# A decoder kernel: the experts' low-rank output in two float32r products instead of one float32 product, and the loading and splitting of its matrix

## The chip, the cores and the metric

The kernel runs on one core of a Trainium2 chip. The metric is the device time of one execution, in microseconds (us). In the profile PE is the matrix engine (TensorE), DVE is VectorE, ACT is ScalarE, POOL is GpSimd, and SP is SyncE, which here only issues DMAs.

## What is computed

Two decoder layers on 1024 tokens of 512 features. Of the six sublayers the third one matters here, a dense layer with experts of low rank: each token picks one of four ranks (8, 16, 32, 64) by its gate scores, and the output of the first that many rows of `A` and columns of `B` is added to the dense product.

```python
def _L0_ffn_ref(hidden_states, W, b, A, B, gate_w, gate_b):
    RANKS = (8, 16, 32, 64)
    out = jnp.einsum('bsd,od->bso', hidden_states, W) + b
    x = hidden_states.reshape(-1, d_in)
    scores = x @ gate_w.T + gate_b
    probs = jax.nn.softmax(scores, axis=-1)
    routing_weights, selected = jax.lax.top_k(probs, TOPK)
    routing_weights = routing_weights / jnp.sum(routing_weights, axis=-1, keepdims=True)
    lora_outputs = jnp.stack([x @ A[:r, :].T @ B[:, :r].T for r in RANKS], axis=1)
    sel = jnp.take_along_axis(lora_outputs, selected[:, :, None], axis=1)
    final = jnp.sum(sel * routing_weights[:, :, None], axis=1)
    return out + final.reshape(bsz, seq, -1)
...
x = _layernorm(x + _L0_attn_ref(...), axis=-1)
x = _layernorm(x + _L0_xattn_ref(ctx_4096, ctx_4096, x), axis=-1)
x = _layernorm(x + _L0_ffn_ref(x, ...), axis=-1)
x = _layernorm(x + _L1_attn_ref(x, ...), axis=-1)
...
```

## The kernel before

Every engine runs a list written out by hand, and the engines meet at semaphores alone; nothing is scheduled. The tokens lie in eight blocks of 128 (`NT` = 8); a block's activations are 128 partitions by 512 columns. A float32 matmul of 512 columns appears in the trace as two records, a float32r one (written F32R, `fp32r` in the trace) as one.

**The second stage** (the second attention, `_L0_xattn`) ends with a loop of t from 0 to 9. Near its end PE already runs `ranks` (L872, the product with `A` and the gate weights, `agT`) and `ffn_W` (L882, the dense product) for blocks 0 and 1. SyncE issues in that loop the keys' rows to DRAM (`keys_out`, L520), scales (L487) and codes (L481) for the quantized weights.

**The third stage** is a loop of t from 0 to 7 on each of PE, ACT and DVE.

On PE, in this order: `lora_T(t)` (L886) turns the 128 x 64 matrix of the chosen rank products; for t < 4, two products of the next layer's low-rank matrices (L901), from t = 3 one of the next layer's combined attention matrix (L912, L913); `ffn_W(t + 2)` up to block 6, and block 7's at t = 7; `ranks(t + 2)`; `lora_out(t)` (L890), which adds the low-rank output and the bias onto the dense product in its bank; and from t = 2 the four transposes of block t - 2 (L606). At t = 7 `attention_out(0)` (L926 to L928, twelve float32r products) stands in as well. There are three banks for the dense product (`FF_BANK`), so `ffn_W(b)` for b of 3 and more waits for `ln_sum`, that is for DVE's addition (L1804) of block b - 3.

On DVE, in each t: from t = 3 the low half of a transposed block (`x_low`, L1810); for t < 4 two additions of the low-rank matrices (L1974); a `stack_low` step at t = 1, 2 and 4 (L1980, L1982, L1987); steps of unpacking the quantized weights (L1739, L1745, L1757, 128 x 1024 each); `choose(t + 2)` (L1960, L1961, L1962, L1965), which turns the gate scores into a mask and multiplies the rank products by it; from t = 3 `m_low` (L1998); then the wait for `lora_out(t)` and the addition and statistics of block t (L1804, L1788, L1789). Inside `choose` each step is "linked": it waits on a semaphore that the one before gives at its end, as each reads what that one wrote.

On ACT, in each t: `lora_T_out(t)` (L1450) copies the turned matrix to `lmT`; the bends of the quantized codes (L1224, L1226, L1232, L1240); `norm_tail` (L1281), which waits for POOL; `m_high_of` (L1440); and `x_T_out` (L1274), which copies a transposed block and is what `x_low` waits for.

PE's transposes of block b wait for `xl_ready` of b, that is for `x_low` of block b - 1 (one bank serves all of them).

Of the kernel before, what the change touches and what calls it, by code (L numbers as in the profile page):

```python
# [11 lines left out]
F32R = mybir.dt.float32r  # L12
# [123 lines left out]
def decoder_kernel(nc, i, out):  # L136
# [4 lines left out]
    with ctx:  # L141
# [28 lines left out]
        ad_st = sb("ad_st", [STACK, FF], F32R)  # L170
        folded_m = sb("folded", [P, T])
# [17 lines left out]
        lmT = sb("lmT", [P, 2, P])  # L189
        probT = lmT  # L190
# [26 lines left out]
        agT, at = carve(arena, at, KD * (RMAX + NL))  # L217
        bT0, at = carve(arena, at, D)
        wk3_at = at
        wk3, at = carve(arena, at, D)  # L220
        bT_d, at = carve(arena, at, D)
        wk2, at = carve(arena, at, D)
# [8 lines left out]
        lm, w_at = carve(early_w, w_at, 2 * RMAX)  # L231
        assert w_at <= 2 * CH
# [4 lines left out]
        lora_l = wo0  # L237
        ad_high = wh[:, :, :].rearrange("p s c -> p (s c)")[:, 0:FF]
# [65 lines left out]
        def turn_bank(n):  # L304

            return bank[(n + 1) % 2]
# [135 lines left out]
        def _(sp):  # L442
# [93 lines left out]
            sp.dma_start(bT0[0:RMAX + 1, :], i["bT0"]).then_inc(in_ffn0, 16)  # L536
# [5 lines left out]
            for t in range(2, NT):  # L542
                keys_out(t)
                if t % 2 == 0:
                    load_scales(C_O + t // 2)
                    load_codes(C_O + 1 + t // 2)
            load_scales(C_O + NT // 2)
# [54 lines left out]
        def _(pe):  # L602
# [259 lines left out]
            def ranks(b):  # L862
                pe.wait_ge(xt_ready, NT + b + 1)
                if b == 0:
                    pe.wait_ge(in_ffn0, 48)
                    pe.wait_ge(kq_ready, NT - 1)
                elif b == 1:
                    pe.wait_ge(kq_ready, NT)
                if b >= 2:
                    pe.wait_ge(lmT_ready, b - 1)  # L870
                for k in range(KD):
                    last = pe.matmul(turn_bank(b)[:, 0:RMAX + NL], xT[:, k, b * P:(b + 1) * P], agT[:, k, :],  # L872
                                     start=(k == 0), stop=(k == KD - 1))
                last.then_inc(ag_ps, 1)
# [343 lines left out]
        def _(act):  # L1218
# [226 lines left out]
            def lora_T_out(b):  # L1445
# [4 lines left out]
                nc.scalar.activation(lmT[0:RMAX, b % 2, :], turn_bank(b)[0:RMAX, P:2 * P], ACT.Copy).then_inc(lmT_ready, 1)  # L1450
# [273 lines left out]
        def _(dve):  # L1724
# [96 lines left out]
            nc.vector.memset(lmT[RMAX:RMAX + 1, :, :], 1.0)  # L1821
# [131 lines left out]
            def choose(b):  # L1953
# [22 lines left out]
            def stack_low_of(part):  # L1976

                dve.wait_ge(stack_hi, part + 1)
# [5 lines left out]
            def down_stack_low():  # L1984

                dve.wait_ge(stack_hi, 4)
                nc.vector.tensor_tensor(ad_st[2 * RG:STACK, :], a_down[2 * RG:STACK, :], f32(ad_high[2 * RG:STACK, :]), ALU.subtract).then_inc(stack_low, 1)  # L1987

            def b_lower(j):

                dve.wait_ge(stack_hi, 4 + j + 1)
# [17 lines left out]
            turn_norm(2 * NT - 1)  # L2009
            choose(1)  # L2010
# [243 lines left out]
def layout(a):  # L2254
# [42 lines left out]
    def pairs(m):  # L2297
# [7 lines left out]
        "bT0": np.concatenate([f["L0_ffn_B"].T[rank_at], f["L0_ffn_b"][None]]), "g_b": np.array([[gate_b[n] for n in LOGITS]], np.float32),  # L2305
# [28 lines left out]
```

## Time and profile before

| | us |
|---|---|
| median of 3 runs | 644.88 |
| the runs | 644.25 to 645.72 |
| the profiled execution | 645.23 |
| its span, first to last instruction | 643.1 |
| PE busy in it | 632.0 |
| DVE busy in it | 396.3 |
| ACT busy in it | 381.6 |

The span is what the trace shows; 2.1 us of the profiled execution lie around it. Busy times are those of each engine by itself; they overlap. In the timelines a DVE operation's length includes its last part, in which the next one may already start if it waits for nothing, so the step from start to start tells what a row takes.

### The profile page before, as it was taken

Reading aid. Unit: us, or ns where it says so; the run is one execution under the profiler, and the core shown is the slowest. Engines: PE = TensorE matmul, PEld = TensorE weight load, DVE = VectorE, ACT = ScalarE, POOL = GpSimd, SP = SyncE. Lnnn points to the kernel's source line nnn. Section 1 sums busy time; section 2 is a strip of 40 time slices with the busy share of each in tenths; the row PEclk is TensorE's granted clock in tenths of the full one; section 3 lists DMA queues with packets and bytes.
Section 4 is the critical chain, followed back from the end, with each engine's and each line's share of the span. In section 5 each row is a group of like instructions: output and inputs, shape, how many; then the busy total and the mean of one; then the engine's idle time right before and its main releaser. Section 6 shows DMA issues by size and latency. Waiting matters only on the chain.

```text
span 643.1 us, 8521 instructions
## 1 busy us (share of the span) xinstructions
PE 632.0 (98%) x3226; PEld 470.0 (73%) x3226; DVE 396.3 (62%) x633; ACT 381.6 (59%) x527; POOL 65.0 (10%) x116
## 2 busy tenths in 40 slices
PE   9999999999999999999999999999999999999996
PEld 6655555544558888888888888887777888888874
DVE  4798787667988777767667355335655212125467
ACT  2977789976987697576675154223565343316532
POOL 1032142311330000000000000001211000000012
PEclk9999999999999999999999999999999999999999
DMA  7771585512253134233320003056010322100002
GB/s 246 288 243 52 188 268 172 162 52 92 81 152 120 39 110 139 73 104 111 94 83 2 1 1 131 1 216 274 1 33 2 115 77 88 33 1 0 1 33 99
DMA packets 25590, 63.92 MB, mean 99 GB/s; under 512 B 5541, under 2 KB 10725, under 8 KB 24782
## 3 DMA queue, kind: packets, MB, share of 16 engines
q1 hardware_dynamic: 23294, 61.68, 29.4%
q10 hardware_dynamic: 2256, 1.70, 0.8%
q8 instruction: 26, 0.43, 0.3%
q14 instruction: 14, 0.11, 0.1%
HBM read 58.77 MB, written 4.60 MB: 99 GB/s over the span
## 4 chain that ended last, share of the span: by engine, by line
PE 88%; DVE 4%; ACT 4%; DMA 1%; issue 1%; SPq 1%; POOL 0%; POOLq 0%; DVEq 0%; ACTq 0%
PE bank L1043 18%; PE bank L1031 8%; PE bank L1030 8%; PE bank L1032 8%; PE bank L1122 8%; PE bank L1121 8%; PE bank L882 4%; PE bank L802 3%; PE bank L606 3%; PE bank L741 2%; PE bank L1097 1%; DMA codes<-in_c_qkv 1%; PE bank L912 1%; PE bank L926 1%; PE bank L984 1%
## 5 line engine op out<-in xcount | busy, mean ns | idle before, releaser
L1232 ACT ACTIVATE line<-line 128x1024 f32<-128x1024 f32 x87 | 91.4, 1050 | 0.2
L1030 PE MATMUL bank<-xh,wh 128*128 128x512 f32 x224 | 87.5, 391 | 0.0
L1031 PE MATMUL bank<-xl,wh 128*128 128x512 f32 x224 | 87.5, 391 | 0.0
L1032 PE MATMUL bank<-xh,wl 128*128 128x512 f32 x224 | 87.3, 390 | 0.0
L1043 PE MATMUL bank<-wh,xh 128*128 128x512 f32 x192 | 76.1, 396 | 0.2 <-DVE xl L2128 0.2
L1043 PE MATMUL bank<-wh,xl 128*128 128x512 f32 x192 | 74.9, 390 | 0.0
L2211 DVE SCALAR_TENSOR_TENSOR arena<-bank,ff_s,arena 128x512 f32<-128x512 f32 x28 | 21.0, 752 | 72.9 <-PE bank L1122 63.8
L2128 DVE TENSOR_TENSOR xl<-arena,xh 128x1024 fp32r<-128x1024 f32 (+1 forms) x26 | 29.7, 1141 | 35.4 <-ACT xh L1536 35.3
L1121 PE MATMUL bank<-xh,wh 128*128 128x512 f32 x128 | 50.3, 393 | 0.0
L1536 ACT ACTIVATE xh<-arena 128x1024 fp32r<-128x1024 f32 (+1 forms) x26 | 25.6, 991 | 41.3 <-PE bank L1043 34.8
L1122 PE MATMUL bank<-xl,wh 128*128 128x512 f32 x128 | 49.9, 390 | 0.0
L1032 PEld LDWEIGHTS bank<-xh,wl 128*128 128x128 f32 x224 | 42.1, 188 | 8.8
L1030 PEld LDWEIGHTS bank<-xh,wh 128*128 128x128 f32 x224 | 42.1, 188 | 8.5
L1031 PEld LDWEIGHTS bank<-xl,wh 128*128 128x128 f32 x224 | 42.1, 188 | 8.5
L1630 ACT ACTIVATE arena<-bank,ff_s 128x512 f32<-128x512 f32 x28 | 19.2, 686 | 43.4 <-PE bank L1122 43.4
L1512 ACT ACTIVATE arena<-bank 128x512 f32<-128x512 f32 x28 | 16.4, 586 | 46.9 <-PE bank L1032 46.9
L1695 POOL TENSOR_TENSOR rstd<-rstd,minus_half 128x1 f32<-128x1 f32 x40 | 26.7, 668 | 172.1 <-DVE rstd L2149 162.4
L1043 PEld LDWEIGHTS bank<-wh,xh 128*128 128x128 f32 x192 | 36.1, 188 | 8.3 <-DVE xl L2128 0.6
L1043 PEld LDWEIGHTS bank<-wh,xl 128*128 128x128 f32 x192 | 36.1, 188 | 7.5
L1121 PE MATMUL bank<-xh,wl 128*128 128x512 f32 x96 | 37.6, 391 | 0.0
L1745 DVE SCALAR_TENSOR_TENSOR line<-line 128x1024 f32<-128x1024 f32 x29 | 35.3, 1218 | 3.6 <-ACT line L1232 3.2
L1043 PE MATMUL bank<-wl,xh 128*128 128x512 f32 x96 | 37.4, 390 | 0.0
(219 smaller groups left out, 1264.3 us busy)
## 6 DMA issues: line engine op xcount, KB each, us to landing
codes<-in_c_gu SPq DMA_DIRECT2D x14, 512.0 KB, 3.8
scales<-in_s_gu SPq DMA_DIRECT2D x28, 256.0 KB, 4.0
codes<-in_t_gu SPq DMA_DIRECT2D x8, 512.0 KB, 4.2
codes<-in_c_dn SPq DMA_DIRECT2D x7, 512.0 KB, 4.6
scales<-in_s_dn SPq DMA_DIRECT2D x14, 256.0 KB, 3.9
fold<-in_t_dn SPq DMA_DIRECT2D x1, 3584.0 KB, 15.7
codes<-in_c_qkv SPq DMA_DIRECT2D x6, 512.0 KB, 4.8
scales<-in_t_gu SPq DMA_DIRECT2D x6, 512.0 KB, 3.8
```

The costliest lines, as they stand in the source:

```text
L882: pe.matmul(bank[FF_BANK[b % 3]][:, :], xT[:, k, b * P:(b + 1) * P], w0T[:, k, :], start=(k == 0), stop=False)
L1030: pe.matmul(dst, wh[:, s, c:c + P], xh[:, k, cols], start=(k == 0), stop=False)
L1031: pe.matmul(dst, wh[:, s, c:c + P], xl[:, k, cols], start=False, stop=False)
L1032: last = pe.matmul(dst, wl[:, s, c:c + P], xh[:, k, cols], start=False, stop=(k == KD - 1))
L1043: ins = pe.matmul(dst, h[:, b * P:(b + 1) * P], w, start=first and p == 0, stop=last and p == len(hiddens) - 1)
L1121: pe.matmul(dst, w[:, c:c + P], xh[:, k, cols], start=(k == 0), stop=False)
L1122: last = pe.matmul(dst, w[:, c:c + P], xl[:, k, cols], start=False, stop=(k == KD - 1))
L1232: nc.scalar.activation(below(slot), below(slot), ACT.Prelu, bias=bias, scale=scale, alpha=alpha).then_inc(bent, 1)
L1536: nc.scalar.activation(dst[:, cols], hT[:, j, cols], ACT.Copy).then_inc(done, 1)
L1695: last = nc.gpsimd.tensor_tensor(rstd[:, m % 2, 1:2], rstd[:, m % 2, 0:1], minus_half[:, :], ALU.pow)
L1745: nc.vector.scalar_tensor_tensor(weight(slot), weight(slot), -NEAR_UP, below(slot), ALU.max, ALU.subtract).then_inc(joined, 1)
L2128: nc.vector.tensor_tensor(low[:, cols], hT[:, j, cols], f32(hi[:, cols]), ALU.subtract).then_inc(done, 1)
```

## The change

The product `lora_out` is made of two float32r products instead of one float32 product. For that both its operands are split into a high part, rounded to float32r, and a low part, the rest.

- DVE: `choose` ends with three linked steps where it had one: the masked product, a cast of it to float32r (`lm_high`), and the difference, so that 128 columns stand side by side: 64 low, 64 high. PE turns all 128 in `lora_T`.
- ACT: `lora_T_out` makes two copies, `lm_both` (128 rows, low above high) and `lm_one` (the high rows again, above rows of ones). Once, before the third stage, it writes the rows of ones (after a wait for the DMAs that send `folded`, whose place `lm_one` takes), and `experts_high` rounds the two stacked copies of the matrix `B`.
- DVE, once: `experts_low`, two subtractions, between `choose(0)` and `choose(1)`.
- PE: `lora_out` is `lm_both` by `b_both` (low by high and high by low) and `lm_one` by `b_high_one` (high by high, and the bias as a high and a low row).
- SyncE: the load of `bT0` (65 x 512) behind `w0T` goes; `b_two` (128 x 512) and `b_one` (97 x 512) are loaded at t = 4 of the second stage's loop, behind `load_codes`.
- The count of `stack_hi` is one higher for all later waits. `lmT` is no longer shared with `probT`.

```diff
@@ block.sync
-            sp.dma_start(bT0[0:RMAX + 1, :], i["bT0"]).then_inc(in_ffn0, 16)
...
+                if t == KD:
+                    sp.dma_start(b_two, i["b_two"]).then_inc(in_ffn0, 16)
+                    sp.dma_start(b_one[0:ONE_ROWS.stop, :], i["b_one"]).then_inc(in_ffn0, 16)
@@ block.tensor
             def ranks(b):
-                    pe.wait_ge(in_ffn0, 48)
+                    pe.wait_ge(in_ffn0, 64)
...
-                pe.transpose(turn_bank(b)[0:RMAX, P:2 * P], lm[:, b % 2, :], ident[:, :]).then_inc(lm_ps, 1)
+                pe.transpose(turn_bank(b)[:, P:2 * P], lm[:, b % 2, :], ident[:, :]).then_inc(lm_ps, 1)
...
             def lora_out(b):
                 pe.wait_ge(lmT_ready, b + 1)
-                pe.matmul(bank[FF_BANK[b % 3]][:, :], lmT[0:RMAX + 1, b % 2, :], bT0[0:RMAX + 1, :], start=False, stop=True).then_inc(f0_ps, 1)
+                if b == 0:
+                    pe.wait_ge(lm_ready, 2)
+                pe.matmul(bank[FF_BANK[b % 3]][:, :], lm_both[:, b % 2, :], b_both, start=False, stop=False)
+                pe.matmul(bank[FF_BANK[b % 3]][:, :], lm_one[0:ONE_ROWS.stop, b % 2, :], b_high_one[0:ONE_ROWS.stop, :], start=False, stop=True).then_inc(f0_ps, 1)
@@ block.scalar
+            def experts_high():
+
+                act.wait_ge(in_ffn0, 64)
+                nc.scalar.activation(b_both, b_two, ACT.Copy)
+                nc.scalar.activation(b_high_one[0:ONE_ROWS.stop, :], b_one[0:ONE_ROWS.stop, :], ACT.Copy).then_inc(stack_hi, 1)
+
             for t in range(1, NT + 2):
+                if t == NT + 1:
+                    experts_high()
...
-                nc.scalar.activation(lmT[0:RMAX, b % 2, :], turn_bank(b)[0:RMAX, P:2 * P], ACT.Copy).then_inc(lmT_ready, 1)
+                nc.scalar.activation(lm_both[:, b % 2, :], turn_bank(b)[:, P:2 * P], ACT.Copy)
+                nc.scalar.activation(lm_one[0:RMAX, b % 2, :], turn_bank(b)[RMAX:P, P:2 * P], ACT.Copy).then_inc(lmT_ready, 1)
+
+            act.wait_ge(kb_out, 16 * KD)
+            for n in range(2):
+                nc.scalar.activation(lm_one[ONE_ROWS, n, :], ident[ONE_ROWS, :], ACT.Identity, bias=1.0, scale=0.0)
@@ block.vector
-            nc.vector.memset(lmT[RMAX:RMAX + 1, :, :], 1.0)
...
-                nc.vector.tensor_tensor(lm[:, s, :].rearrange("p (r m) -> p r m", m=SEG), ps[:, 0:RMAX].rearrange("p (r m) -> p r m", m=SEG),
-                                        mask.unsqueeze(1).to_broadcast([P, RMAX // SEG, SEG]), ALU.mult).then_inc(lm_ready, 1)
+                chosen, high = lm[:, s, 0:RMAX], lm_high[:, s, RMAX:P]
+                link(nc.vector.tensor_tensor(chosen.rearrange("p (r m) -> p r m", m=SEG), ps[:, 0:RMAX].rearrange("p (r m) -> p r m", m=SEG),
+                                             mask.unsqueeze(1).to_broadcast([P, RMAX // SEG, SEG]), ALU.mult))
+                link(nc.vector.tensor_copy(high, chosen))
+                nc.vector.tensor_tensor(chosen, chosen, f32(high), ALU.subtract).then_inc(lm_ready, 1)
+
+            def experts_low():
+
+                dve.wait_ge(stack_hi, 1)
+                low, row = slice(RMAX, P), slice(RMAX + ROWG, RMAX + ROWG + 1)
+                nc.vector.tensor_tensor(b_both[low, :], b_two[low, :], f32(b_both[low, :]), ALU.subtract)
+                nc.vector.tensor_tensor(b_high_one[row, :], b_one[row, :], f32(b_high_one[row, :]), ALU.subtract)
...
             choose(0)
             turn_norm(2 * NT - 1)
+            experts_low()
             choose(1)
```

The order of the instructions on the engines, at the places that matter. On DVE, t = 0 of the third stage, `choose(2)` and the addition of block 0, before:

```order
L1960 TENSOR_TENSOR gate_v<-bank,g_b 128x48 [waits ag_ps]
L1961 TENSOR_REDUCE gate_v<-gate_v 128x16 [waits dve_step]
L1962 TENSOR_TENSOR gate_v<-gate_v 128x8 [waits dve_step]
L1965 TENSOR_TENSOR early_w<-bank,gate_v 128x64 [waits lm_ps,dve_step]
L1804 TENSOR_TENSOR rbuf<-x,bank 128x512 [waits ln_done,f0_ps]
L1788 BN_STATS st<-rbuf 128x6 [waits ln_sum]
L1789 BN_AGGR mv<-st 128x2 [waits dve_step]
```

and in the changed kernel, where `early_w` is the place of `lm` and `wl` that of `lm_high`:

```order
L1987 TENSOR_TENSOR gate_v<-bank,g_b 128x48 [waits ag_ps]
L1988 TENSOR_REDUCE gate_v<-gate_v 128x16 [waits dve_step]
L1989 TENSOR_TENSOR gate_v<-gate_v 128x8 [waits dve_step]
L1993 TENSOR_TENSOR early_w<-bank,gate_v 128x64 [waits lm_ps,dve_step]
L1995 CAST wl<-early_w 128x64 [waits dve_step]
L1996 TENSOR_TENSOR early_w<-early_w,wl 128x64 [waits dve_step]
L1832 TENSOR_TENSOR rbuf<-x,bank 128x512 [waits ln_done,f0_ps]
L1816 BN_STATS st<-rbuf 128x6 [waits ln_sum]
L1817 BN_AGGR mv<-st 128x2 [waits dve_step]
```

The cast and the subtraction stand between the masked product and the addition of block 0, and the cast and the subtraction each wait for the step ahead of them. The same holds at each of the eight `choose` steps.

On PE, the third stage from `ranks(2)` to the dense product of block 3, before:

```order
L872 MATMUL bank<-arena 128x112 [waits lmT_ready,xt_ready]
L872 MATMUL bank<-arena 128x112 x3
L890 MATMUL bank<-arena,lmT 128x512 [waits lmT_ready]
L886 MATMUL bank<-ident,early_w 64x128 [waits lm_ready]
L901 MATMUL bank<-early_w,arena 128x512 [waits af_added]
L901 MATMUL bank<-early_w,arena 128x512
L882 MATMUL bank<-arena 128x512 [waits ln_sum]
```

and in the changed kernel (`early_w` under `ident` is the matrix that `lora_T` turns):

```order
L884 MATMUL bank<-arena 128x112 [waits lmT_ready,xt_ready]
L884 MATMUL bank<-arena 128x112 x3
L904 MATMUL bank<-arena_r,lm_both 128x512 [waits lm_ready,lmT_ready]
L905 MATMUL bank<-arena_r,lm_one 128x512
L898 MATMUL bank<-ident,early_w 128x128 [waits lm_ready]
L916 MATMUL bank<-early_w,arena 128x512 [waits af_added]
L916 MATMUL bank<-early_w,arena 128x512
L894 MATMUL bank<-arena 128x512 [waits ln_sum]
```

The one product on `lmT` became two, and block 0's waits for `lm_ready` too; the rest stands as it stood.

On ACT, the end of the second stage and the start of the third, before:

```order
L1274 ACTIVATE arena<-bank 128x4x128 [waits xt_ps]
L1232 ACTIVATE line<-line 128x1024 [waits bent]
L1274 ACTIVATE arena<-bank 128x4x128 [waits xt_ps]
L1450 ACTIVATE lmT<-bank 64x128 [waits lm_ps]
L1224 ACTIVATE line<-codes 128x1024 [waits joined,in_codes0]
```

and in the changed kernel:

```order
L1289 ACTIVATE arena<-bank 128x4x128 [waits xt_ps]
L1247 ACTIVATE line<-line 128x1024 [waits bent]
L1403 ACTIVATE arena_r<-arena 128x512 [waits in_ffn0]
L1404 ACTIVATE arena_r<-arena 97x512
L1289 ACTIVATE arena<-bank 128x4x128 [waits xt_ps]
L1478 ACTIVATE lm_one<-ident 33x128 [waits kb_out]
L1478 ACTIVATE lm_one<-ident 33x128
L1473 ACTIVATE lm_both<-bank 128x128 [waits lm_ps]
L1474 ACTIVATE lm_one<-bank 64x128
L1239 ACTIVATE line<-codes 128x1024 [waits joined,in_codes0]
```

`experts_high` stands ahead of the copy of block 7's transposes, the rows of ones behind it, ahead of `lora_T_out(0)`.

## Rows read from the trace of the kernel before

**Rows 1.** The page's busy time of each engine: time, share of the span, instructions.

```profile
PE 632.0 (98%) x3226; PEld 470.0 (73%) x3226; DVE 396.3 (62%) x633; ACT 381.6 (59%) x527; POOL 65.0 (10%) x116
```

**Rows 2.** Stretches of the third stage: length, busy time by engine, PEclk, DMA.

```profile
137.30:161.00 23.70, 23.70 (x85) 11.54 (x84) 19.27 (x36) 17.55 (x23) 4.95 (x9) 1.00 0.30 90
161.00:182.50 21.50, 21.36 (x78) 11.31 (x76) 20.53 (x36) 20.83 (x27) 7.09 (x8) 1.00 0.34 103
...
190.00:216.50 26.50, 26.22 (x138) 21.41 (x137) 22.01 (x32) 18.15 (x29) 0.79 (x2) 1.00 0.36 105
```

**Rows 3.** The chain of waits, 118 to 220 us: start, length, what.

```profile
137.31 0.87 PE bank L890 x2
138.30 1.06 PE bank L901 x4
139.36 3.63 PE bank L882 x8
...
187.88 0.23 PE bank L928
```

**Rows 4.** DVE's timeline at block 2's choice: start, length, operation [idle before].

```profile
137.35 0.21 DVE L1960 TENSOR_TENSOR gate_v<-bank,g_b 128x48 f32<-128x48 f32 x1 [0.71 <-PE bank L872]
...
137.83 0.17 DVE L1962 TENSOR_TENSOR gate_v<-gate_v 128x8 f32<-128x8 f32 x1
138.03 0.22 DVE L1965 TENSOR_TENSOR early_w<-bank,gate_v 128x64 f32<-128x64 f32 x1
138.22 0.69 DVE L1804 TENSOR_TENSOR rbuf<-x,bank 128x512 f32<-128x512 f32 x1
```

**Rows 5.** The same timeline of DVE at blocks 3 and 4.

```profile
142.92 1.23 DVE L1739 SCALAR_TENSOR_TENSOR line<-line 128x1024 f32<-128x1024 f32 x1
144.06 0.20 DVE L1960 TENSOR_TENSOR gate_v<-bank,g_b 128x48 f32<-128x48 f32 x1
...
151.52 0.68 DVE L1804 TENSOR_TENSOR rbuf<-x,bank 128x512 f32<-128x512 f32 x1
152.23 0.69 DVE L1788 BATCH_NORM_STATS2 st<-rbuf 128x6 f32<-128x512 f32 x1
```

**Rows 6.** PE's timeline, the dense product of block 5.

```profile
152.83 3.70 PE L882 MATMUL bank<-arena 128*128 128x512 f32 x8
```

**Rows 7.** DVE's timeline from 156 to 182 us.

```profile
156.14 1.23 DVE L1745 SCALAR_TENSOR_TENSOR line<-line 128x1024 f32<-128x1024 f32 x1
161.10 0.21 DVE L1960 TENSOR_TENSOR gate_v<-bank,g_b 128x48 f32<-128x48 f32 x1 [3.73 <-PE bank L872]
...
168.37 2.02 DVE L1987 TENSOR_TENSOR ad_st<-a_down,wh 32x1792 fp32r<-32x1792 f32 x1
170.49 0.21 DVE L1960 TENSOR_TENSOR gate_v<-bank,g_b 128x48 f32<-128x48 f32 x1
...
177.64 0.20 DVE L1960 TENSOR_TENSOR gate_v<-bank,g_b 128x48 f32<-128x48 f32 x1
...
181.71 0.68 DVE L1810 TENSOR_TENSOR xl<-bank,xh 128x512 fp32r<-128x512 f32 x1
```

**Rows 8.** PE's timeline, the transposes of block 4 at 182 us.

```profile
182.54 0.63 PE L606 MATMUL bank<-ident,x 128*128 128x128 f32 x4 [0.19 <-DVE xl L1810]
```

**Rows 9.** DVE's groups by form: busy time and mean ns of one.

```profile
L1844 DVE COPY project<-bank 128x64 f32<-128x64 f32 x8 | 1.2, 215 | 0.0
...
L1817 DVE COPY fold<-ident 128x128 f32<-128x128 f32 x1 | 0.2, 227 | 0.0
```

**Rows 10.** Timeline of ACT at 131 us.

```profile
131.67 0.60 ACT L1274 ACTIVATE arena<-bank 128x512 f32<-128x512 f32 x1 [3.23 <-PE bank L606]
```

**Rows 11.** Timeline of DVE, the idle stretch before 132.9 us.

```profile
132.89 1.28 DVE L1974 TENSOR_TENSOR arena<-arena,bank 128x512 f32<-128x512 f32 x2 [4.20 <-PE bank L901]
```

**Rows 12.** SyncE's own queue: when its DMAs were issued.

```profile
106.88 0.57 SPq L481 DMA_DIRECT2D codes<-in_c_dn  x1
111.38 5.26 SPq L520 DMA_DIRECT2D kq<-heads  x2
```

More of the change, by code:

```diff
@@ L170, in decoder_kernel @@
         ad_st = sb("ad_st", [STACK, FF], F32R)
+        with nc.sbuf_tensor("lm_one", [P, T], F32R) as lm_one:
+            pass
         folded_m = sb("folded", [P, T])
@@ L188, in decoder_kernel @@
         gate_v = sb("gate_v", [P, 2, NL + 3 * SEG])
-        lmT = sb("lmT", [P, 2, P])
-        probT = lmT
+        with nc.sbuf_tensor("lm_both", [P, 2, P], F32R) as lm_both:
+            pass
+        probT = sb("probT", [P, 2, P])
         prob = sb("prob", [P, 2, P])
@@ L217, in decoder_kernel @@
         agT, at = carve(arena, at, KD * (RMAX + NL))
+        b_low_at = at
         bT0, at = carve(arena, at, D)
@@ L221, in decoder_kernel @@
         bT_d, at = carve(arena, at, D)
+        b_high_at = at
         wk2, at = carve(arena, at, D)
@@ L230, in decoder_kernel @@
         s_qkv, w_at = carve(early_w, w_at, 3 * KD * NB)
-        lm, w_at = carve(early_w, w_at, 2 * RMAX)
-        assert w_at <= 2 * CH
+        lm = early_w[:, FF:2 * CH]
+        assert w_at <= 2 * CH and 2 * CH - FF == 4 * RMAX and 2 * RMAX == P
+        lm_high = wl[:, :, :].rearrange("p s c -> p (s c)")[:, FF:2 * CH].rearrange("p (s c) -> p s c", s=2)
         qkT, wv, lm = qkT.rearrange("p (j c) -> p j c", j=KD), wv.rearrange("p (j c) -> p j c", j=KD), lm.rearrange("p (s c) -> p s c", s=2)
@@ L237, in decoder_kernel @@
         lora_l = wo0
+        b_two, b_one = wk3, m_free[:, 0:D]
+        b_both, b_high_one = arena_r[:, b_low_at:b_low_at + D], arena_r[:, b_high_at:b_high_at + D]
+        ONE_ROWS = slice(RMAX, RMAX + ROWG + 1)
+        lm_one = lm_one[:, 0:2 * P].rearrange("p (s t) -> p s t", s=2)
         ad_high = wh[:, :, :].rearrange("p s c -> p (s c)")[:, 0:FF]
@@ L1976, in stack_low_of @@
             def stack_low_of(part):
-                dve.wait_ge(stack_hi, part + 1)
+                dve.wait_ge(stack_hi, 1 + part + 1)
                 if part == 0:
@@ L1984, in down_stack_low @@
             def down_stack_low():
-                dve.wait_ge(stack_hi, 4)
+                dve.wait_ge(stack_hi, 1 + 4)
                 nc.vector.tensor_tensor(ad_st[2 * RG:STACK, :], a_down[2 * RG:STACK, :], f32(ad_high[2 * RG:STACK, :]), ALU.subtract).then_inc(stack_low, 1)
             def b_lower(j):
-                dve.wait_ge(stack_hi, 4 + j + 1)
+                dve.wait_ge(stack_hi, 1 + 4 + j + 1)
                 part = b_st[RG:2 * RG, j % 2, :]
@@ L2304, in layout @@
         "w0T": rows(c(f["L0_ffn_W"].T)), "agT": rows(np.concatenate([f["L0_ffn_A"][rank_at].T, np.stack([gate_w[n] for n in LOGITS], 1)], 1)),
-        "bT0": np.concatenate([f["L0_ffn_B"].T[rank_at], f["L0_ffn_b"][None]]), "g_b": np.array([[gate_b[n] for n in LOGITS]], np.float32),
+        "b_two": np.concatenate([f["L0_ffn_B"].T[rank_at]] * 2),
+        "b_one": np.concatenate([f["L0_ffn_B"].T[rank_at], f["L0_ffn_b"][None], np.zeros((ROWG - 1, D), np.float32), f["L0_ffn_b"][None]]), "g_b": np.array([[gate_b[n] for n in LOGITS]], np.float32),
         "c_qkv": pairs(ca[:3].reshape(3 * KD, P, D)), "c_o": pairs(ca[3].T.reshape(KD, P, D)),
```

## The prediction

> **What bounds the kernel now.** I read the page's busy times first: PE works in 632.0 of 643.1 us [rows 1], so what is taken from PE ought to come off the end, unless something else comes late there. Then the stretches of the third stage, where every edit lies [rows 2]. PE is busy in all of 137.3 to 161.0 us. But DVE is busy for 19.27 of those 23.70 us and idle in one piece for 3.73 at their end [rows 7]; that leaves 0.7 us idle in the rest, nearly all before its first row. From 161.0 to 182.5 DVE is busy for 20.53 of 21.50 and ACT for 20.83. So two engines run level with PE here, and the sum has to be made on both sides. The chain of waits shows PE up to about 170 us, then DVE's rows, and it comes back to PE at 182.54, where the transposes of block 4 waited 0.19 us for DVE's `x_low` [rows 8].
>
> **What PE gains.** `lora_out` takes 0.87 us, in two records [rows 3]. A float32r product of the same width takes 0.23 [rows 3], two take 0.46. That is 0.41 less in each of eight rounds, 3.3 us in all. The transpose of 128 columns in place of 64 moves the same 128 columns of the identity through the array; I take nothing for it; PE runs four such transposes in 0.63 with the wait for their start [rows 8].
>
> **What DVE pays.** In a round before, from the start of the masked product to the addition is 138.22 - 138.03 = 0.19 us [rows 4]. A linked step costs its length and 0.03: 137.83 + 0.17 = 138.00, and the next starts at 138.03 [rows 4]. After the change the masked product is linked, 0.22 + 0.03. The cast of 64 columns has no row of its own. A copy of 64 columns from a bank takes 0.215, one of 128 columns between SBUF tiles 0.227 [rows 9], the step on 8 columns 0.17 [rows 4]; I take 0.20, and 0.03 for the link. The subtraction of 64 columns, whose end overlaps the addition, takes 0.17, between the 0.15 to 0.19 of the old last step. The new total is 0.65, and c, what a round adds on DVE, is 0.46. Its bounds: 0.36 (0.17 for the cast, 0.12 for the subtraction's step) and 0.56 (0.227, and a subtraction seen whole at 0.24).
>
> By a rule of the Trainium skill, page "VectorE: DVE Perf Modes", section "The perf-mode tier table", a float32 copy between SBUF tiles goes at twice the rate and a float32 `tensor_tensor` does not. With that page's fixed part of 151 cycles, an estimate is 0.19 us for the cast and 0.22 for the subtraction. The 0.22 agrees with L1965 [rows 4]. At 0.19 the sum below would be lower by 6 x 0.01, under 0.1 us; at the whole rate, as the bank copy, higher by the same.
>
> **How the two meet, first half.** DVE's addition of block b - 3 releases the dense product of block b. DVE starts `choose(2)` when PE's `ranks(2)` ends, at 137.35 [rows 4], as before. The addition of block 0 then comes 0.44 later (c, less 0.02 for a wait on PE that it had). The rows behind stand back to back: L1739 starts at 142.92 and `choose(3)` at 144.06, one step of such a row [rows 5], and there is no idle time to take the delay up. So block 1's addition is 2c late and block 2's, at 151.52, 3c less 0.04, which is 1.34. It took 0.68, and DVE's result reached PE 0.15 after its end at 182.39 [rows 7, 8], so block 5's dense product could have started at 152.35 and started at 152.83 [rows 6]: 0.48 to spare. Now it starts 1.34 - 0.48 = 0.86 later. PE has saved 3 x 0.41 by then, and all of it turns into waiting at the dense products of blocks 3, 4 and 5.
>
> **Second half.** From there to `ranks(5)` PE works through, so `choose(5)`, at 161.10 after 3.73 us of idle time [rows 7], is 0.86 late too: the idle time hid what DVE owed, but not what PE now owes. Then DVE is full again. L1987 ends at 170.39 and `choose(6)` starts at 170.49 [rows 7], 0.1 to spare; `choose(7)` follows at 177.64, and `x_low` of block 3 at 181.71. Three more rounds make it 0.86 + 3 x 0.46 - 0.1 = 2.14 late. PE's transposes of block 4 wait for it already [rows 8], so PE is 2.14 late there, whatever `lora_out(3)` to `(6)` saved. That wait grows from 0.2 to about 2 us.
>
> **Third part.** Behind it DVE has idle time again and PE works through up to 216.5, with 0.28 us idle in 26.5 [rows 2]. `lora_out(7)` gives back 0.41, less 0.02 for small waits. The stage ends 2.14 - 0.39 = 1.75 us later; in c this is 6c - 1.0. The gate and up products that follow are PE's alone, so it stays to the end.
>
> **The parts that cost nothing.** `experts_high` is two ACT rows of the kind of the 128 x 512 copy, 0.60 each, in ACT's idle 3.23 us before 131.67 [rows 10]. `experts_low` starts behind it at about 129.5, two subtractions of 512 columns, 0.68 each as `x_low` [rows 7]; `choose(1)` follows and ends near 132.0, inside DVE's 4.20 us of idle time before 132.89 [rows 11]. Without that cover they would cost 1.3 us and 0.9. The new wait of `lora_out(0)` on `choose(1)` is over 5 us before it matters. The rows of ones and the second copy add 0.2 to 0.3 us each on ACT; the copies of rounds 4 to 6 make `lmT_ready(6)` some 0.5 later than PE's delay at that place, which falls into the 2 us wait. ACT's wait for the beta rows' DMAs has queued behind it only ACT's first copy and bends, with some microseconds to spare before `ranks(3)`. On SyncE the two loads are issued after the codes of 106.88 and before 111.38, when it next has something to do [rows 12]: two issues of about 0.6, in a queue that stands waiting for 4 us, and more than 8 us before `ranks(0)` needs them. Cost 0. Their bounds: to each side 0.3 us, for what a later landing of the codes could do.
>
> **The sum.** 645.23 + 1.75 = 647.0 for the profiled execution. It lies 0.35 above the median of the runs, so the median is 646.6.
>
> **Rivals.**
> 1. *PE's gain arrives* (faster). If DVE's added rows hid behind the waits for PE, the end would come 3.3 us earlier: 641.6. For it speaks that PE is at 98%; against it, that DVE has 0.7 us idle where it would need 1.4, and that the addition cannot pass the new rows in DVE's own queue.
> 2. *The two nearly cancel* (no change). It needs c of 0.15 to 0.37, a cast and a subtraction that cost hardly more than their steps of start; at 0.25, 6c - 1.0 is 0.5 us: 645.4. The formula turns at c = 0.17, below that it is faster. Against it, each link costs a whole length, as in all of `choose`.
> 3. *The clock falls in the new wait* (slower still). The granted clock is 1.00 (2.4 GHz) in all three stretches, and PE's waits there are 0.3 us or less [rows 2]. The new wait of 2 us has no like in them. If the clock fell to 1.2 GHz behind it, the dense product of block 7 would take twice its 3.63 [rows 3]: 1.75 + 3.6, 650.2. The page "TensorE: Matmul & The Clock Gate" of the Trainium skill, part 1, says that an idle array is gated to half its clock; no row here shows PE idle long enough to tell.
> 4. *ACT becomes the bound* (slower). It is busy for 20.83 of 21.50 us [rows 2], and gets 0.2 to 0.3 more in each round and a later start. If a bend is what DVE's L1739 then waits for, a further 1 us: 647.6.
>
> **How the numbers follow.** The forecast, c from 0.38 to 0.6, 61%; rival 1, 8%; rival 2, 20%; rival 3, 4%; rival 4, 7%. A measurement tells about 0.2%, 1.3 us, from no change. Slower by more than that (over 646.2) is the forecast but for its low edge, with rivals 3 and 4: 0.66. Within it is rival 2 and the low edge, less its part below: 0.25. Faster is rival 1 and a little of 2: 0.09. The range: c of 0.25 to 0.56 with the 0.3 of the hidden parts gives 645.1 to 647.5; taking in rival 4 and the rest of rival 2 it is 644.5 to 648.2, and leaves out rivals 1 and 3 and some of each edge.
>
> **What would show it.** Two float32r records of 0.23 in place of two of 0.43. DVE's step from the masked product to the addition near 0.65. PE waiting for DVE's addition (`rbuf`) at the dense products of blocks 3 to 5, 0.4 to 0.9 us each, and about 2 us for `xl` at block 4's transposes. The third stage 1.75 longer as a whole, and no stretch behind 216.5 changed. It is wrong if PE shows no wait on DVE before 170 us, if c is under 0.35, or if the clock is below 1.00 after 184.

## The result, and the profile after

| | before | after |
|---|---|---|
| median, us | 645.22 (5 runs) | 648.46 (5 runs) |
| lowest to highest | 644.25 to 645.72 | 646.80 to 650.10 |
| ratio | | 1.0048, 95% interval 1.0037 to 1.0060 |
| the profiled execution, and its span | 645.23, 643.1 | 646.80, 644.9 |
| third stage: `choose(2)` on DVE to the first gate product on PE | 78.91 | 81.42 |

The kernel is slower by 3.2 us. The same kernel run again in the study gave 647.53 (647.41 to 649.11, 5 runs; ratio 1.0045, 1.0033 to 1.0058), with a stage of 81.40 us. Two executions of the study in a slower state, one of the kernel before at 709.73 us (mean granted clock 0.851) and one of the run without the split at 1280.37 us, are in no ratio and no count below, and they move a median by 0.12 us at most. The profiled execution of the first set is its shortest: it entered the stage 0.8 us earlier than that of before did. So the stage is measured from its own start, `choose(2)` on DVE: 137.35 us before, 136.55 after. Behind the stage nothing changed: from the first gate product to the end of the span are 426.8 us before and 426.9 after.

PE does less and the rest more than in [rows 1]. The page after:

```profile
PE 628.8 (98%) x3226; PEld 469.4 (73%) x3226; DVE 400.6 (62%) x650; ACT 386.8 (60%) x539; POOL 65.0 (10%) x116
```

PE lost 3.2 us of busy time and the span grew by 1.8. Of the 3.2, 0.8 lie ahead of the stage and 2.4 in it. The stretches that answer to [rows 2], cut at the waits (length, then busy time of PE, PEld, DVE, ACT and POOL, then PEclk and DMA):

```profile
136.50:160.20 23.70, 21.88 (x78) 10.78 (x77) 20.49 (x42) 18.93 (x26) 4.96 (x9) 1.00 0.31 89
160.20:182.30 22.10, 20.67 (x85) 12.12 (x84) 20.17 (x40) 21.42 (x30) 5.53 (x7) 1.00 0.34 100
182.30:189.60 7.30, 6.01 (x22) 3.44 (x21) 5.59 (x8) 6.29 (x10) 3.29 (x4) 1.00 0.60 157
189.60:218.00 28.40, 27.61 (x145) 22.42 (x143) 23.72 (x33) 18.82 (x30) 2.59 (x4) 1.00 0.34 97
```

Where PE was busy for all of the first 23.70 us it now idles for 1.82, and in the next two stretches for 1.43 and 1.29. The timeline of PE names who it waits for (start, length, operation, in brackets the idle time before it and its releaser):

```profile
138.60 3.70 PE L894 MATMUL bank<-arena 128*128 128x512 f32 x8 [0.43 <-DVE rbuf L1832]
...
145.74 3.70 PE L894 MATMUL bank<-arena 128*128 128x512 f32 x8 [0.92 <-DVE rbuf L1832]
...
176.35 0.63 PE L618 MATMUL bank<-ident,x 128*128 128x128 f32 x4 [0.21 <-DVE xl L1838]
...
181.97 0.50 PE L904 MATMUL bank<-arena_r,lm_both 128*128 128x512 f32 x1 [1.23 <-ACT lm_one L1474]
182.31 0.39 PE L905 MATMUL bank<-arena_r,lm_one 97*128 97x512 f32 x1
183.98 0.63 PE L618 MATMUL bank<-ident,x 128*128 128x128 f32 x4 [1.29 <-DVE xl L1838]
...
195.12 0.63 PE L618 MATMUL bank<-ident,x 128*128 128x128 f32 x4 [0.48 <-DVE xl L1838]
```

The dense product of block 5, at 152.87, waited 0.47 for the same row. Together that is 5.0 us of waits where [rows 8] had one of 0.19. The rows of the choice on DVE, to set beside [rows 4]:

```profile
137.23 0.22 DVE L1993 TENSOR_TENSOR early_w<-bank,gate_v 128x64 f32<-128x64 f32 x1
137.49 0.20 DVE L1995 CAST wl<-early_w 128x64 fp32r<-128x64 f32 x1
137.72 0.23 DVE L1996 TENSOR_TENSOR early_w<-early_w,wl 128x64 f32<-128x64 f32 x1
137.86 0.68 DVE L1832 TENSOR_TENSOR rbuf<-x,bank 128x512 f32<-128x512 f32 x1
```

From the masked product to the addition it is now 137.86 - 137.23 = 0.63 us where it was 0.19. So c is 0.44.

### The profile page after: what moved, and what is told of

It is laid out like the page before. It is cut to its first block, busy times and chain, and to the rows that moved or that the text cites. A ratio compares the mean times of both kernels' runs of the same rounds, so it can differ in the third digit from the quotient of the medians.

```text
span 644.9 us, 8552 instructions
## 1 busy us (share of the span) xinstructions
PE 628.8 (98%) x3226; PEld 469.4 (73%) x3226; DVE 400.6 (62%) x650; ACT 386.8 (60%) x539; POOL 65.0 (10%) x116
## 4 chain that ended last, share of the span: by engine, by line
PE 84%; DVE 7%; ACT 4%; issue 2%; POOL 1%; DMA 1%; POOLq 0%; DVEq 0%; ACTq 0%
PE bank L1058 18%; PE bank L1046 8%; PE bank L1045 8%; PE bank L1047 8%; PE bank L1137 8%; PE bank L1136 8%; PE bank L814 3%; PE bank L618 3%; PE bank L753 2%; PE bank L894 2%; PE bank L1112 1%; PE bank L641 1%; PE bank L730 1%; PE bank L999 1%; ACT line L1247 1%
```

## The experiments

Starts below are counted from `choose(2)` of the same trace, as "block 4's transposes at 47.4". In before they stand at 45.19, block 5's at 52.86, block 6's at 56.10; after at 47.43, 54.69 and 58.57. Each run has its ratio to the kernel before on the same chip, with its 95% interval.

### The kernel after, again

> The changed kernel again, for a second trace and five more times. Theory A (DVE's added rows): its third stage, from the start of choose(2) to the first gate product, takes 81.4 us as in the first trace (78.9 in the kernel before), whatever the whole takes, and PE waits on DVE's addition three times (1.8 us in all). The first trace gained 0.8 us ahead of that stage; if that was luck of that one execution, this one starts the stage up to 0.8 us later and the time is +2.5 us (647.7); if it belongs to the change, +1.8 (647.0). Rival: the clock falls behind the new waits: then the granted clock shows under 1.00 between 182 and 195 us in one of the executions, and the times spread by over 2 us.

647.53 us, as told above. Every wait of PE comes back within 0.02 us (0.44, 0.91, 0.47, 0.20, 1.22, 1.30, 0.46), though the stage began 0.8 us later. So the waits belong to the kernel. The early start did not come back; the trace of after is the only one of the study in which the stage begins before 136.9 us.

### DVE's steps alone, on the kernel before

```diff
-                nc.vector.tensor_tensor(lm[:, s, :]..., ALU.mult).then_inc(lm_ready, 1)
+                link(nc.vector.tensor_tensor(chosen..., ALU.mult))
+                link(nc.vector.tensor_copy(high, chosen))
+                nc.vector.tensor_tensor(rest, chosen, f32(high), ALU.subtract).then_inc(lm_ready, 1)
```

> The kernel before with only the two further linked steps on DVE in each choice (the cast and a subtraction into a spare tile); PE, ACT and the loads as before. Theory A: each round costs DVE 0.44 us, PE gets nothing back, so block 4's transposes come 6 x 0.44 - 0.6 = 2.0 to 2.3 us later and nothing is returned at the last lora_out: +2.3 to +2.9 us. Rival B (the new waits or the two ACT copies are the cause, not DVE's rows): +0.5 or less. Rival C (PE's float32r gain would be lost anyway): this one has no gain to lose and ends within 0.3 us of the changed kernel.

647.99 us, ratio 1.0050 (1.0038 to 1.0062): two linked rows in each round, whose results nobody reads, cost about as much as the whole change. Block 4's transposes start at 47.77, 2.6 late, which is above the 2.0 to 2.3 that were expected: here DVE itself waited 0.46 us for a bend of ACT, which it does neither before nor after (DVE's timeline).

```profile
168.62 1.23 DVE L1746 SCALAR_TENSOR_TENSOR line<-line 128x1024 f32<-128x1024 f32 x1 [0.46 <-ACT line L1233]
```

The product is still the float32 one, and PE waited only 0.33 us for ACT's copy, so the wait for `x_low` is 1.33. Behind it this trace shows more (PE's timeline and its stretches of 2 us):

```profile
182.51 1.12 PE L891 MATMUL bank<-arena,lmT 65*128 65x512 f32 x2 [0.33 <-ACT lmT L1451]
184.96 0.63 PE L607 MATMUL bank<-ident,x 128*128 128x128 f32 x4 [1.33 <-DVE xl L1811]
```

```profile
184.00:186.00 2.00, 1.04 (x6) 1.01 (x7) 1.95 (x3) 1.19 (x2) 1.82 (x3) 0.86 0.18 51
186.00:188.00 2.00, 2.00 (x3) 0.67 (x2) 0.56 (x1) 1.89 (x3) 0.08 (x1) 0.50 0.88 252
188.00:190.00 2.00, 2.00 (x5) 0.90 (x4) 1.93 (x5) 2.00 (x5) 0.24 (x1) 0.78 0.71 270
```

The granted clock fell to 0.50 (1.2 GHz) behind the wait, and the dense product of block 7 took 5.22 us where it takes 3.60. This stage took 83.17 us. From block 4's transposes to block 5's it is 9.36 us where before has 7.67, so an estimate of the stage without the fall is 83.17 - 1.69 = 81.5, as in after. In the traces of after and of its repetition the same stretches read 1.00. The prediction's third rival therefore exists, in some executions; a later section counts them.

### The change without the split on DVE

The masked product is rounded to float32r as it is written, and the low part stays zero (it is set once in each of the first two rounds): `lm_both` by `b_both` adds only high by low.

```diff
-                link(nc.vector.tensor_tensor(chosen..., ALU.mult))
-                link(nc.vector.tensor_copy(high, chosen))
-                nc.vector.tensor_tensor(chosen, chosen, f32(high), ALU.subtract).then_inc(lm_ready, 1)
+                if b < 2:
+                    link(nc.vector.memset(chosen, 0.0))
+                nc.vector.tensor_tensor(high..., ALU.mult).then_inc(lm_ready, 1)
```

> The changed kernel without the cast and the subtraction: the masked product is written as the high part at once and the low part stays zero, so the output lacks the low part of the chosen rank products. ACT's two copies, the rows of ones, the loads and both float32r products stay. Theory A: DVE's chain is as long as before the change, so PE's gain shows up to what DVE had to spare: 0.4 to 1.2 us faster than the kernel before. Rival B (ACT's copies or the waits cost the time): still 1.5 us or more slower than before. Rival D (PE's 3.3 us all arrive): 3 us faster.

645.39 us, ratio 1.0003 (0.9994 to 1.0012), stage 78.68. The loss is gone, and the cast and subtraction are shown to be its cause from both sides. But PE's gain hardly appears either: 0.2 us in the stage, out of 8 x 0.40 (below), where 0.4 to 1.2 were expected. The timelines of PE, ACT and DVE at the place:

```profile
181.55 0.50 PE L904 MATMUL bank<-arena_r,lm_both 128*128 128x512 f32 x1 [1.27 <-ACT lm_one L1474]
181.89 0.39 PE L905 MATMUL bank<-arena_r,lm_one 97*128 97x512 f32 x1
182.66 0.63 PE L618 MATMUL bank<-ident,x 128*128 128x128 f32 x4 [0.38 <-DVE xl L1838]
```

```profile
178.42 2.14 ACT L1247 ACTIVATE line<-line 128x1024 f32<-128x1024 f32 x2
180.47 0.58 ACT L1289 ACTIVATE xh<-bank 128x512 fp32r<-128x512 f32 x1
180.94 0.27 ACT L1473 ACTIVATE lm_both<-bank 128x128 fp32r<-128x128 f32 x1
181.22 0.27 ACT L1474 ACTIVATE lm_one<-bank 64x128 fp32r<-64x128 f32 x1
```

```profile
180.71 1.21 DVE L1785 SCALAR_TENSOR_TENSOR fold<-line,scales 128x1024 f32<-128x1024 f32 x1
181.83 0.68 DVE L1838 TENSOR_TENSOR xl<-bank,xh 128x512 fp32r<-128x512 f32 x1
```

None of these rows of ACT and DVE has idle time in front: both engines are full here even without the added rows. PE waits 1.27 us for ACT's second copy, and then 0.38 for `x_low`. The second wait is the one that counts: ACT's copy that `x_low` reads had ended at 181.05, and `x_low` stood behind an unpacking step in DVE's own queue until 181.83. By this timeline, earlier copies alone would only have made PE wait longer for `x_low`. So what PE saves in rounds 3 to 6 is lost to DVE's queue, as the prediction's second half has it. Further on, at block 6's transposes, PE waits 0.46 for `x_low` again, over the path of the section after next.

### The split on POOL

The complete computation; cast and subtraction go to POOL, which was 10% busy. (The lines on DVE, where the masked product is now the last step, are left out here.)

```diff
+            def split(b):
+                chosen, high = lm[:, b % 2, 0:RMAX], lm_high[:, b % 2, RMAX:P]
+                pool.wait_ge(chosen_made, b + 1)
+                link(nc.gpsimd.tensor_copy(high, chosen))
+                nc.gpsimd.tensor_tensor(chosen, chosen, high.bitcast(F32), ALU.subtract).then_inc(lm_ready, 1)
```

> The changed kernel with the cast and the subtraction moved to POOL, whose queue takes them ahead of the next rstd step; the computation is whole. Theory A: DVE gets its 0.44 us a round back, lora_T needs the split two rounds later only, so as e3: 0.4 to 1.2 us faster than before. Rival E: POOL's steps (0.3 to 0.6 us each, two a round) delay the rstd steps that ACT's norm_tail and then x_low wait for in the last rounds: 0.5 to 1 us slower than e3.

645.61 us, ratio 1.0008 (1.0000 to 1.0017), stage 78.69, the waits of the run before to 0.01 us. POOL's rows read longer than DVE's (the profile's lengths on POOL are rough), and cost nothing in the stage, since PE turns the matrix a dense product later:

```profile
138.77 0.24 POOL L1746 CAST wl<-early_w 128x64 fp32r<-128x64 f32 x1 [5.79 <-DVE early_w L2006]
139.08 0.32 POOL L1747 TENSOR_TENSOR early_w<-early_w,wl 128x64 f32<-128x64 f32 x1
```

What the change pays on DVE is thus a matter of where the rows stand, not that they exist.

### Block 5's copy ahead of a bend

In the prediction's third part DVE's delay was to have ended at block 4, with 0.41 given back by `lora_out(7)`. After shows a wait of 0.48 at block 6's transposes instead. Here ACT, at t = 7, copies block 5's transposes ahead of the bend and the rest of that half step.

```diff
+                if t == NT - 1:
+                    x_T_out(2 * NT + t - 2, dst=xh)
                 for u, h in half_plan(3, t, 1):
...
-                if t >= 2:
+                if 2 <= t < NT - 1:
```

> The changed kernel with one swap in ACT's last round (t = 7): the copy of block 5's transposes stands ahead of the bend behind norm_tail, where it stood after it. It tests the term that the prediction took as 0.02. Theory F (the wait of 0.48 us for x_low at block 6's transposes comes from DVE's delay, by POOL, norm_tail and one bend, and is not given back): x_low comes 1.0 us earlier, the wait goes, and the stage from choose(2) to the first gate product takes 80.8 to 80.9 us in place of 81.4. Rival G (something else is late next, the bend for DVE's join among others): 81.3 to 81.5.

647.99 us, ratio 1.0042 (1.0027 to 1.0056). Stage 80.72, 0.7 less than after, and no wait at block 6's transposes; `x_low` follows ACT's copy at once:

```profile
192.32 0.82 ACT L1296 ACTIVATE x<-rbuf,rstd 128x512 f32<-128x512 f32 x1 [1.50 <-POOL rstd L1728]
193.16 0.60 ACT L1289 ACTIVATE xh<-bank 128x512 fp32r<-128x512 f32 x1
```

The stage confirms the wait as the missing 0.7 us. The median of the times doesn't by itself (its interval overlaps that of after); the three executions with a mean clock of 0.999, a choice made afterwards, point the same way, at 646.40 to 646.98 against 647.41 to 648.46 for the three of after and its repetition.

### Products that fill the two waits

Two float32 products whose result nobody reads stand in PE's two long waits of t = 6.

```diff
+                if t == 6:
+                    pe.wait_ge(m_low, 3)
+                    pe.matmul(bank[4][:, :], ident[:, :], x[:, 0, :], start=True, stop=True)
                 lora_out(t)
+                if t == 6:
+                    pe.matmul(bank[4][:, :], ident[:, :], x[:, 0, :], start=True, stop=True)
```

> The changed kernel with two float32 products of 512 columns (0.87 us each) into a free bank, one ahead of lora_out(6) and one behind it, where PE waited 1.2 and 1.3 us in the traces. They compute nothing that is used. Theory H (in about half of the executions the clock falls behind these waits, which makes the time 648.2 to 650.1 in place of 647.4): the stage stays at 81.4 to 81.5 us, no execution shows a mean clock under 0.997, and all times lie within 0.8 us of 647.5. Rival I (the low clocks have another cause): the same two groups as before, a median of 647.5 to 648.5.

> e7 once more for five more executions, on whether the filler keeps the clock up. Theory H: again none under a mean clock of 0.997, times 647.4 to 648. In the kernels with a PE wait of 1.2 us or more and no filler (the changed kernel, e1, e2, e3, e5, e6) 13 of 44 executions were at 0.996 or less. Rival I: one to three of the five at 0.996 or less.

647.84 us (647.59 to 649.07, 5 runs), and in the second set 647.81 (647.59 to 647.91, 6 runs); ratios 1.0040 (1.0027 to 1.0053) and 1.0034 (1.0022 to 1.0045). The stage stays, 81.37 and 81.39. The waits shrink to 0.21 and 0.42 (the second set's PE):

```profile
181.72 1.13 PE L977 MATMUL bank<-x,ident 128*128 128x512 f32 x2
183.06 0.50 PE L904 MATMUL bank<-arena_r,lm_both 128*128 128x512 f32 x1 [0.21 <-ACT lm_one L1479]
183.64 1.02 PE L980 MATMUL bank<-x,ident 128*128 128x512 f32 x2
185.08 0.63 PE L618 MATMUL bank<-ident,x 128*128 128x128 f32 x4 [0.42 <-DVE xl L1843]
```

The median doesn't move by an amount that can be told. One time, 649.07, lies outside the 0.8 us that were expected, at a mean clock of 0.998: it is the profiled one of the first set, and its stage began at 138.91 us, 1.26 later than that of the second set, so the excess arose ahead of the stage. The mean clocks are counted in the section on the clock.

### The moved load alone, on the kernel before

```diff
-            sp.dma_start(bT0[0:RMAX + 1, :], i["bT0"]).then_inc(in_ffn0, 16)
...
+                if t == KD:
+                    sp.dma_start(bT0[0:RMAX + 1, :], i["bT0"]).then_inc(in_ffn0, 16)
```

> The kernel before with its load of bT0 moved to t = 4 of the second stage's loop, behind the codes, and nothing else. All theories: within 0.3 us of the kernel before, and choose(2) starts where it did. A rival in which the moved load delays the codes or the keys' rows: 0.5 us or more slower, with an idle stretch of ACT or DVE before 125 us.

645.48 us, ratio 1.0001 (0.9992 to 1.0009), stage 78.89. Moving the load behind the codes costs nothing.

### Another order at the end of the stage

If ACT's and DVE's order near t = 5 to 7 decides what PE's gain is worth, an order that puts the copy of a transposed block and its `x_low` first, and copies block 6's matrix one round early, should show it. The same lines went onto the POOL version, the kernel before and the kernel after.

```diff
             for t in range(NT):
-                lora_T_out(t)
+                if t != 6:
+                    lora_T_out(t)
...
+                if t >= 5:
+                    x_T_out(2 * NT + t - 2, dst=xh)
+                if t == 5:
+                    lora_T_out(t + 1)
                 for u, h in half_plan(3, t, 1):
...
-                if t >= 3:
+                if 3 <= t < 6:
                     x_low(2 * NT + t - 3)
...
+                elif t >= 5:
+                    x_low(2 * NT + t - 2)
```

> e5 (the split on POOL) with the last rounds ordered anew: from t = 5 on ACT copies the transposed block ahead of its second bends, and the turned matrix of round 6 right behind that; on DVE x_low of blocks 3 and 4 stands ahead of the unpacking step that it followed. The computation is whole. Theory A with F: PE's waits at lora_out(6) and at the transposes of blocks 4 and 6 (1.3, 0.4 and 0.5 us) shrink, the stage takes 77.2 to 77.8 us (78.7 in e5, 78.9 before), and the kernel is 1.0 to 1.6 us faster than before. Rival G: the unpacking, which is now later, becomes what the gate product waits for: 78.5 or more.

> The kernel before with only e9's order of the last rounds (ACT's copies and DVE's x_low ahead of the second bends and the second unpacking step), its float32 product as it was. It tells whether e9's 1.0 us come from the order alone. Theory A with F: before, PE waited 0.19 us for x_low in this stage and nowhere else but at its end, so the order is worth 0.2 us: stage 78.6 to 78.8 us, time within 0.4 us of before; the split on POOL with the float32r products is what makes the rest of e9. Rival J: the order alone gives 1 us (stage 77.8).

> The changed kernel, its split still on DVE, with e9's order. Theory A with F: block 4's transposes come 1.1 us earlier than in the changed kernel (x_low no longer behind one unpacking step) and block 6's wait goes too: stage 79.4 to 79.9 us (81.4 in the changed kernel, 78.9 before), still slower than before by 0.5 to 1 us. Rival K (the order mends all of it): 78.9 or less.

| the order on | us | ratio (95%) | stage | stage without it |
|---|---|---|---|---|
| the POOL version | 644.29 | 0.9984 (0.9975 to 0.9992) | 77.75 | 78.69 |
| before | 645.13 | 0.9992 (0.9983 to 1.0000) | 78.53 | 78.91 |
| after | 646.82 | 1.0023 (1.0014 to 1.0031) | 80.46 | 81.42 |

The first beats both kernels, by 1.0 us against the kernel before. On before the order alone is worth 0.4 in the stage and can hardly be told in the time. So 0.8 us of the stage are PE's gain, which arrives once neither DVE's added rows nor the old order stand in front of it. At block 4 it is the order on DVE that helps: the transposes start 1.1 us earlier than without it on the POOL version (43.57 against 44.71) and 1.2 on after (46.27 against 47.43), about one unpacking step, which `x_low` now has behind it. Most of the rest of PE's 3.2 is again waiting, in four waits. Three of them (PE's timeline of the first; the fourth is 0.16 at block 6's transposes):

```profile
145.19 3.70 PE L895 MATMUL bank<-arena 128*128 128x512 f32 x8 [0.41 <-DVE rbuf L1850]
...
180.56 0.63 PE L619 MATMUL bank<-ident,x 128*128 128x128 f32 x4 [0.77 <-DVE xl L1856]
...
184.97 0.51 PE L942 MATMUL bank<-m_hi,xh 128*128 128x512 f32 x1 [0.24 <-DVE arena_r L2051]
```

On after the order takes ACT's wait away (1.23) and the wait for `x_low` grows from 1.29 to 1.63, for the same reason: `x_low` was the later of the two. The stage of 80.46 lies above the 79.4 to 79.9 that were expected for it.

## Where the prediction was right and where it failed

**The mechanism was right.** DVE's linked rows became the bound, and PE's gain became waiting. c was forecast 0.46 and is 0.44. The three dense products wait 0.43, 0.92 and 0.47 for the addition, within 0.02 of the range of 0.4 to 0.9 that was named. Block 4's transposes were to be 2.14 late and are 2.24. PE's gain was forecast 0.41 a round and is 0.40 (PE's timeline of round 3, before and after):

```profile
142.82 1.04 PE L872 MATMUL bank<-arena 128*128 128x112 f32 x8
143.70 1.04 PE L890 MATMUL bank<-arena,lmT 65*128 65x512 f32 x2
144.58 0.27 PE L886 MATMUL bank<-ident,early_w 128*64 128x128 f32 x1
```

```profile
142.13 1.04 PE L884 MATMUL bank<-arena 128*128 128x112 f32 x8
142.94 0.47 PE L904 MATMUL bank<-arena_r,lm_both 128*128 128x512 f32 x1
143.26 0.39 PE L905 MATMUL bank<-arena_r,lm_one 97*128 97x512 f32 x1
143.49 0.27 PE L898 MATMUL bank<-ident,early_w 128*128 128x128 f32 x1
```

From the start of `ranks` to that of the next transpose it is 1.76 us before and 1.36 after. The first float32r record takes 0.32 to the start of the next, not 0.23, but it starts 0.81 behind the start of `ranks`, where the float32 one started 0.88 behind it. Where PE doesn't wait in either trace, as from block 5's dense product to block 6's, the stretch shrinks from 13.15 to 12.76. That the moved load costs nothing is shown by its own run. The two ACT rows of `experts_high` and DVE's `experts_low` stand in idle time, with 0.57 us of it left (timeline of DVE after, beside [rows 11]), and the two runs without the added rows in DVE's rounds keep them and lose nothing:

```profile
129.42 0.69 DVE L2003 TENSOR_TENSOR arena_r<-arena,arena_r 1x512 fp32r<-1x512 f32 x1
...
131.29 0.22 DVE L1996 TENSOR_TENSOR early_w<-early_w,wl 128x64 f32<-128x64 f32 x1
132.09 1.28 DVE L2011 TENSOR_TENSOR arena<-arena,bank 128x512 f32<-128x512 f32 x2 [0.57 <-PE bank L916]
```

**The step that failed: "`lora_out(7)` gives back 0.41, less 0.02 for small waits".** The stage was to end 2.14 - 0.39 = 1.75 later; it ends 2.5 later. The give-back is real as far as block 5's transposes, which are 54.69 - 52.86 = 1.83 late. But those of block 6 are 58.57 - 56.10 = 2.47 late, after a wait of 0.48 for `x_low`, a term that the prediction put at 0.02 among its small waits. The prediction looked at DVE's idle time and at PE's, and left out the path that passes by both: DVE's statistics to POOL (`rstd`), ACT's `norm_tail`, a bend, the copy of block 5's transposes, `x_low`. After:

```profile
188.66 0.18 DVE L1817 BATCH_NORM_AGGREGATE mv<-st 128x2 f32<-128x6 f32 x1
...
194.28 0.69 DVE L1838 TENSOR_TENSOR xl<-bank,xh 128x512 fp32r<-128x512 f32 x1 [0.86 <-ACT xh L1289]
```

```profile
190.79 1.03 POOL L1726 TENSOR_SCALAR rstd<-mv,rstd 128x1 f32<-128x1 f32 x1
191.86 0.82 ACT L1296 ACTIVATE x<-rbuf,rstd 128x512 f32<-128x512 f32 x1 [1.50 <-POOL rstd L1726]
```

In the trace of before:

```profile
187.07 0.18 DVE L1789 BATCH_NORM_AGGREGATE mv<-st 128x2 f32<-128x6 f32 x1
...
192.55 0.69 DVE L1810 TENSOR_TENSOR xl<-bank,xh 128x512 fp32r<-128x512 f32 x1 [0.32 <-ACT xh L1274]
```

```profile
190.28 0.82 ACT L1281 ACTIVATE x<-rbuf,rstd 128x512 f32<-128x512 f32 x1 [1.80 <-POOL rstd L1698]
```

From `choose(2)` the statistics' last row is at 49.72 before and 52.11 after, `norm_tail` at 52.93 and 55.31, `x_low` at 55.20 and 57.73: 2.4 to 2.5 late all along. Block 6's transposes start 0.90 behind `x_low` without a wait before and 0.84 behind it after a wait now, so the path had 0.06 us to spare. For PE to keep its 1.83 it would have needed 0.70, the difference to `x_low`'s 2.53, and nearly the whole of DVE's delay reached PE a second time. The run with the copy first took it off, and the stage became 80.72; that is 1.8 over before, near the 1.75 of the sum.

**The base.** The 0.35 us by which the profiled execution lay above the median came from three runs. The kernel before has its median at 645.22 to 645.38 beside each group of runs of this study, so this step should have been about zero. Base and stage make 0.35 + 0.75 = 1.1 of the 1.9 us between the forecast median, 646.6, and 648.46. The rest is how the executions of the first set fell, which no trace explains: the second set's median, 647.53, lies inside the range, so whether a set of five falls in or out of it was partly luck.

**A rival priced alone.** The falling clock had a chance of 4% and was kept apart from the forecast; as the next section counts it, it is rather an addition, in a part of the executions. Its price, 3.6 us for a whole dense product at half the clock, was too high: the one fall in a trace cost 1.69. The sum with base and stage put right is 645.3 + 2.5 = 647.8. The ten executions of after and its repetition have their median at 648.3.

**The ends of the range.** The high end, 648.2, was made of c's bounds and the ACT rival, and no term stood for waits behind 184.

**The other points.** ACT's copies of round 6 were to be 0.5 late; `lora_T_out(6)` started 1.9 late (181.36 after, 180.28 before) and PE waited 1.23 for it, since `norm_tail` in front of it was itself 1.7 late (177.50, released by POOL, and 176.56 before): the same path, one block earlier. This is hidden, as `x_low` comes later still, in after and in the third experiment. The "about 2 us" for `xl` was one of 1.29 with that 1.23 ahead of it. "PE's gain arrives" is refuted for this kernel, and even with DVE's added rows taken out 0.2 of 3.2 us arrive.

## How often the clock falls

Only one trace caught a fall. For the other executions there is only the mean granted clock, and it is a rough sign: the trace with the fall has a mean of 0.997, which executions of every group reach without being slow, so the counts of 0.996 or less leave out falls as short as that one. The counts, over all runs of the study that have a clock on record:

| kernels | PE's longest wait in the stage, us | executions | mean clock 0.996 or less |
|---|---|---|---|
| before | 0.3 | 69 | 1 |
| load alone; order on before; order on POOL version | 0.8 | 34 | 0 |
| with filling products | 0.9 | 11 | 0 |
| after (10), DVE's steps (6), no split (10), split on POOL (11), copy first (7), order on after (12) | 1.2 to 1.6 | 56 | 14 |

Of after and its repetition the four executions at 0.996 or less took 648.17 to 650.10 (median 648.8), the six others 646.80 to 648.76 (median 647.5). With the waits filled, eleven executions lie between 647.59 and 649.07, ten of them within 0.34 us. So low clocks went along with PE waits of 1.2 us and more, in a quarter of executions, and those executions of after were about 1.3 us longer. That the waits are the cause is not shown. At a rate of one in four, eleven filled executions without a low clock would come about by chance once in 24 times (an estimate, 0.75 to the eleventh power), and of twelve executions with the new order on after, with a wait of 1.63, one had a low clock. Nor is the clock the whole of the scatter: at clocks of 1.00 in the traces the stage begins anywhere from 136.55 to 138.91 us. The Trainium skill, page "TensorE: Matmul & The Clock Gate", part 1, says that an idle array is gated to half its clock; the trace of DVE's steps shows 0.50, behind waits of 0.33 and 1.33 us and while PE was busy again. Where the clock fell in the executions of after with a low mean is open, and so is why the same waits leave it at 1.00 in most.

## What to carry to other kernels

Before shortening the fullest engine, count the idle time of the one that releases it, and price each row that the change adds to a linked chain there at its whole length, once a round. Follow a delay down every path that leaves the delayed engine, the small ones over POOL and ACT too, up to the last place where two of them meet again; idle time on the engine that you look at says nothing about a path that goes around it. In this kernel the small rows cost nothing on an engine with idle time, POOL, and the order of the engines that PE waits for had to be changed with them before a part of the saving arrived. Where two waits of one engine stand one behind the other, ask which of the two releasers is the later: the earlier one alone is not what holds the engine, as the timelines of the third experiment show.

## What the runs showed that was not expected

- Waits of 0.33 and 1.33 us with 1.1 us of work between them were followed by a granted clock of 0.50 in one trace: a dense product took 5.22 us in place of 3.60.
- A float32r record of 512 columns takes 0.23 us from start to start among its like, and 0.32 as the first behind float32 ones. Two of them in place of a float32 product still save 0.40 us, as the first one starts 0.07 sooner behind the records ahead of it.
- On POOL, whose lengths are rough in the profile, a cast of 128 x 64 read 0.24 us and a subtraction 0.32, beside 0.20 and 0.23 on DVE.
- The same seven waits of PE came back within 0.02 us in two executions that entered the stage 0.8 us apart.
